# A gated cross-attention and expert layer: queries completed on TensorE, the last chunk's output path in two halves

## The reference

```
x = x + tanh(g_xattn) * attention(layernorm(x), ctx, ctx)      # 8 heads of 4 columns, softmax over 1601 keys, then Wo, bo
x = x + tanh(g_ffn)   * experts(layernorm(x))

experts(x2): scores = softmax(x2 @ router_w + router_b)        # 8 experts
             G, idx = top_k(scores.T, 512)                     # each expert takes its 512 best rows
             h1 = relu(x2[idx] @ w1 + b1);  eo = h1 @ w2 + b2  # 256 -> 1024 -> 256
             y[idx] += eo * G
```

## Time and profile before

| | |
|---|---|
| median of 3 runs | 636.62 us (634.16 to 638.63) |
| the profiled execution | 634.5 us, of which its span is 632.7 us |
| busy in the span | TensorE 542.0 us (86%), VectorE 449.5 (71%), ScalarE 387.8 (61%), GpSimd 187.8 (30%) |
| VectorE's maxima, L866 | 256 reductions, 243.2 us |
| mean granted TensorE clock | 0.928 of 2.4 GHz |

### The profile page before, as it was taken

One profiled execution on the slowest core, in us unless ns is written; L12 is line 12 of the kernel. 1 busy time (PEld: TensorE's weight loads), 2 busy tenths in 40 slices (PEclk: granted clock), 3 DMA queues, 4 the chain that ended last, 5 costly groups with the idle time before them and its releaser, 6 DMA issues.

```text
span 632.7 us, 12435 instructions
## 1 busy us (share of the span) xinstructions
PE 542.0 (86%) x4879; PEld 326.5 (52%) x4879; DVE 449.5 (71%) x815; ACT 387.8 (61%) x742; POOL 187.8 (30%) x184
## 2 busy tenths in 40 slices
PE   5876999989999899999889843369999999999991
PEld 3421333334334343433334332249898898898981
DVE  4789979997798987989895037735767667666630
ACT  1673878876888768888687810025646646655641
POOL 3053420040510315100092001050526437346223
PEclk9995999998999999999899955559999999999996
DMA  7600000000000000000000050021446347346123
GB/s 265 221 2 1 1 1 2 2 2 34 2 35 1 3 34 1 35 2 1 35 36 1 1 171 29 2 66 34 142 122 137 102 108 188 98 107 157 20 26 33
DMA packets 23469, 35.74 MB, mean 56 GB/s; under 512 B 3411, under 2 KB 16116, under 8 KB 23284
## 3 DMA queue, kind: packets, MB, share of 16 engines
q1 hardware_dynamic: 17268, 26.56, 12.6%
q0 software_dynamic: 6144, 8.39, 7.6%
HBM read 26.56 MB, written 8.39 MB: 55 GB/s over the span
## 4 chain that ended last, share of the span: by engine, by line
PE 58%; DVE 23%; issue 5%; ACT 5%; POOL 1%; DMA 0%; POOLq 0%; DVEq 0%; ACTq 0%
DVE mquart L866 16%; PE ps L1424 14%; PE ps L1431 14%; PE ps L1265 9%; PE ps L1235 5%; PE ps L1252 4%; ACT probs L647 3%; PE ps L1172 2%; PE ps L1383 1%; PE ps L1302 1%; PE ps L1288 1%; PE ps L1397 1%; PE ps L1406 1%; DVE stats L775 1%; PE ps L1273 1%
## 5 line engine op out<-in xcount | busy, mean ns | idle before, releaser
L866 DVE TENSOR_REDUCE mquart<-ps 128x2 f32<-128x802 f32 x256 | 243.2, 988 | 23.5 <-PE ps L1235 18.1
L647 ACT ACTIVATE probs<-ps 128x512 f32<-128x512 f32 (+1 forms) x416 | 222.3, 598 | 57.1 <-PE ps L1252 56.0
L1265 PE MATMUL ps<-probs,vp 128*32 128x256 f32 (+1 forms) x1664 | 135.1, 397 | 4.3 <-ACT osb L556 4.3
L1235 PE MATMUL ps<-kpad,qrows 64*128 64x401 bf16 x512 | 91.8, 346 | 15.2 <-DVE mquart L866 14.3
L1113 DVE TENSOR_TENSOR h1l<-hf,h1h 128x512 fp32r<-128x512 f32 x64 | 44.1, 689 | 72.5 <-ACT hf L721 72.5
L1252 PE MATMUL ps<-qfull,kpad 64*128 64x256 bf16 (+1 forms) x832 | 89.1, 278 | 1.7 <-ACT xf L569 0.6
L720 ACT ACTIVATE h1h<-ps,b1T 128x512 fp32r<-128x512 f32 x64 | 44.0, 687 | 62.9 <-PE ps L1424 62.8
L1431 PE MATMUL ps<-w2h,h1h 128*128 128x256 f32 x256 | 73.8, 288 | 1.4 <-DVE h1l L1113 0.7
L1431 PE MATMUL ps<-w2l,h1h 128*128 128x256 f32 x256 | 72.4, 283 | 0.0
L1431 PE MATMUL ps<-w2h,h1l 128*128 128x256 f32 x256 | 72.3, 283 | 0.0
L1235 PEld LDWEIGHTS ps<-kpad,qrows 64*128 64x128 bf16 x512 | 26.2, 94 | 76.8 <-DVE mquart L866 39.3
(11 more groups left out here) (163 smaller groups left out, 677.8 us busy)
## 6 DMA issues: line engine op xcount, KB each, us to landing
w1raw<-in_L_ffn_w SPq DMA_DIRECT2D x16, 512.0 KB, 4.1
w2raw<-in_L_ffn_w SPq DMA_DIRECT2D x16, 512.0 KB, 4.5
xs<-in_x SPq DMA_DIRECT2D x4, 512.0 KB, 8.7
out<-xs SPq DMA_DIRECT2D x4, 512.0 KB, 2.6
x_rows<-x SPq DMA_DIRECT2D x4, 512.0 KB, 2.6
ctx_sb<-in_ctx SPq DMA_DIRECT2D x3, 512.0 KB, 6.8
b2b<-in_L_ffn_b SPq DMA_DIRECT2D x1, 1024.0 KB, 11.6
toks<-x_rows,idx_get POOLq DMA_INDIRECT x32, 2.8
```

The source lines that it names most:

```text
L647: nc.scalar.activation(out_p, ps[0:w, next_bank(), :], ACT.Exp, scale=float(SCALE)).then_inc(s_ex, 1)
L866: nc.vector.tensor_reduce(mquart[:, t, a, :, kq], ps[:, b:b + 2, 0:MAXW], AX.X, ALU.max).then_inc(s_mr, 1)
L1235: last = mm(ps[:, bank + b, 0:MAXW], qrows[band(b), g, q:q + P], kpad[band(b), g, a, lo:lo + MAXW], start=True, stop=True)
L1265: last = mm(ps[32 * hh:32 * hh + 32, PV, 0:UW], vp[0:w, kt, g, hh, :], probs[0:w, step % PROBS, hh, :], start=(kt == 0), stop=(kt == NKT - 1))
```

## The change

- `place_max` first multiplies the identity with qrows into the bank (bf16, 256 columns) and adds the transposed maxima on top; `q_full` becomes a ScalarE copy. The placing uses one of ScalarE's three banks.
- `max_parts` reduces twice, into mparts (bf16) and into nmax, instead of reducing once and copying; mquart has two buffers.
- Unit 0 follows the first 16 maxima at once; its loop spreads 20 tiles instead of 16 (`tiles_by(0, i)`).
- wo and the router of chunks 0 to 2 run in two halves at two steps, in ScalarE's banks. ScalarE scales wo's result into x2 (`scale_wo`), GpSimd adds it to x (`add_wo`); ScalarE takes the logits (`take_L`), GpSimd adds the router's bias (`add_rb`).
- LayerNorm-1 statistics of chunks 1 and 2 move before the first maxima, with their rstd on GpSimd ahead of add_bo(0); those of chunk 3, and LayerNorm-2's, are spread over four steps.
- One key projection and the query projection of group 1 are cut in two, with a maximum between.
- The last chunk's output path runs in two halves of two tiles: the first inside the last unit (HALF_O and the names beside it give the steps; the transposing of b1 goes there too), the second behind it. Its stores come in halves.

```diff
+            if u == 0:
+                return TILES + (tiles_by(1, -1) - TILES) * (i + 1) // (2 * NKT)
             return min(TILES * UNITS, TILES * (u + 1) + TILES * (i + 1 + 2 * LEAD) // (2 * NKT))
 
...
-        O_THIS, O_LAST, BACK_AT, WO_AT = (2, 4), (0, 4), (0, 7), (0, 10)
+        O_THIS, O_LAST, BACK_AT, WO_AT = (2, 4), (0, 4), (0, 7), ((0, 10), (0, 12))
...
-        X2_AT, ROUTER_AT = ((2, 6), (2, 8)), (2, 11)
+        X2_AT, ROUTER_AT = ((2, 6), (2, 8)), ((2, 10), (2, 12))
+        LAST = NC - 1
+        HALF_O, HALF_BACK, HALF_WO, HALF_B1, HALF_X2, HALF_ROUTER = [(UNITS - 1, k) for k in (2, 3, 5, 8, 10, 12)]
...
+            for half in range(2):
+                t = CT * LAST + UQ * half
+                sp.wait_ge(s_x1, LAST + half + 1)
+                sp.dma_start(out_v[:, t:t + UQ, :], xs[:, t:t + UQ, :]).then_inc(s_out1, 16)
+                sp.wait_ge(s_x2, LAST + half + 1)
+                sp.dma_start(x2_v[:, t:t + UQ, :], x2[:, UQ * half:UQ * half + UQ, :]).then_inc(s_x2st, 16)
...
+            def add_rb(c):
+
+                pool.wait_ge(s_rwts, 64)
+                pool.wait_ge(s_lgr, 2 * (c + 1))
+                rows = lg[:, CT * c:CT * c + CT, :]
+                nc.gpsimd.tensor_tensor(rows, rows, rbb[:, :].unsqueeze(1).to_broadcast([P, CT, E]), ALU.add).then_inc(s_lg, 1)
...
+            def add_wo(c):
+
+                pool.wait_ge(s_xb, c + 1)
+                pool.wait_ge(s_wt, 2 * (c + 1))
+                rows = xs[:, CT * c:CT * c + CT, :]
+                nc.gpsimd.tensor_tensor(rows, rows, x2[:, :, :], ALU.add).then_inc(s_x1, 1)
...
+            rstd_1(1)
+            rstd_1(2)
             pool.wait_ge(s_bob, 1)
             add_bo(0)
...
                 if c + 1 < NC:
-                    rstd(c + 1, mv1, rstd1, s_mv1, s_ve1, s_rs1)
+                    if c + 1 == NC - 1:
+                        rstd_1(c + 1)
                     ln1_apply(c + 1)
                     add_bo(c + 1)
+                if c > 0:
+                    add_wo(c - 1)
+                if c + 1 < NC:
...
+                    rstd_2(c - 1)
                     ln2_apply(c - 1)
+                if 0 < c < LAST:
+                    add_rb(c - 1)
             first_weights()
-            rstd(NC - 1, mv2, rstd2, s_mv2, s_ve2, s_rs2)
+            add_rb(LAST - 1)
+            for half in range(2):
+                rstd_2(LAST, half)
...
+            def q_full(u):
+
+                c, g, h, r = unit(u)
+                act.wait_ge(s_mpl, u + 1)
+                at_least(act, s_sc, 2 * NKT * (u + 1 - PER_CHUNK))
+                take(qfull[:, g, UW * h:UW * h + UW], ps[:, next_bank(), 0:UW], s_qf)
+
+            def scale_wo(c, half, bank):
+
+                act.wait_ge(s_W, 2 * c + half + 1)
+                act.wait_ge(s_x2st, 16 * (c + 1))
+                at_least(act, s_X, KD * c)
+                nc.scalar.activation(x2[:, 2 * half:2 * half + 2, :], ps[:, bank, :].rearrange("p (t d) -> p t d", d=D), ACT.Copy,
+                                     scale=tg[:, 0:1]).then_inc(s_wt, 1)
+
...
+            def take_L(c, half, bank):
+
+                act.wait_ge(s_R, 2 * c + half + 1)
+                t = CT * c + UQ * half
+                take(lg[:, t:t + UQ, :], ps[:, bank, 0:UQ * E].rearrange("p (t e) -> p t e", e=E), s_lgr)
...
+                    if kt == PLACE and u + 1 < UNITS:
+                        q_full(u + 1)
...
-            take_N(NC - 1, 4)
+            take_N(LAST, 1, 4)
             take(iota_x[:, :, :], cst[:, C_IOTA:C_IOTA + P].unsqueeze(2).to_broadcast([P, P, QT]), s_iota)
-            for k in range(KD):
-                take_X(NC - 1, k, k)
+            take_X_half(1, 0)
...
+                if j == 0:
+                    for t in range(CT):
+                        ln1_stats(1, t)
+                if j == 1:
+                    ln1_aggr(1)
+                    ln1_stats(2, 0)
+                if j == 2:
+                    for t in range(1, CT):
+                        ln1_stats(2, t)
+            ln1_aggr(2)
             split(4, 0, CW, 0, qrows[:, 0, 0:CW])
...
-                nc.vector.tensor_reduce(nmax[:, :, :].rearrange("p t (b a) -> p t a b", a=2), mquart[:, :, :, :, :], AX.X, ALU.max,
+                at_least(dve, s_mpl, u)
+
+                def spread(t, row):
+                    return t[:, :, :, row].rearrange("p t (b a) -> p t a b", a=2)
+
+                nc.vector.tensor_reduce(spread(mparts, KROW_M), mquart[:, u % 2, :, :, :, :], AX.X, ALU.max, negate=True)
+                nc.vector.tensor_reduce(nmax[:, :, :].rearrange("p t (b a) -> p t a b", a=2), mquart[:, u % 2, :, :, :, :], AX.X, ALU.max,
                                         negate=True).then_inc(s_nm, 1)
                 dve.wait_ge(s_nm, u + 1)
-                at_least(dve, s_mpl, u)
-                nc.vector.tensor_copy(mparts[:, :, :, KROW_M], nmax[:, :, :]).then_inc(s_mhi, 1)
-                dve.wait_ge(s_mhi, u + 1)
                 nc.vector.tensor_tensor(mparts[:, :, :, KROW_M + 1], nmax[:, :, :], mparts[:, :, :, KROW_M], ALU.subtract).then_inc(s_mp, 1)
...
-                nc.vector.tensor_tensor(qfull[:, g, UW * h:UW * h + UW], ps[:, next_bank(), 0:UW], qrows[:, g, a:a + UW], ALU.add).then_inc(s_qf, 1)
...
-                nc.vector.scalar_tensor_tensor(rows, ps[:, bank:bank + 2, :].rearrange("p b (t d) -> p (b t) d", d=D), tg[:, 0:1], rows,
...
-            for n in range(TILES, TILES + 2):
-                max_tile(n)
-            q_full(0)
-            for n in range(TILES + 2, TILES + EARLY):
-                max_tile(n)
...
-                    if c > 0 and r == 1 and kt == 1:
-                        ln2_stats(c - 1, FIRST2)
-                    if c > 0 and r == 1 and kt == 2:
-                        ln2_stats(c - 1, LAST2)
-                    if c > 0 and r == 1 and kt == 3:
+                        normalise(c - 1, 1, 0, next_bank())
+                    if c > 0 and (r, kt) in LN2_AT:
+                        ln2_stats(c - 1, LN2_AT.index((r, kt)))
+                    if c > 0 and (r, kt - 1) == LN2_AT[-1]:
                         ln2_aggr(c - 1)
...
+                    if c + 1 == NC - 1 and (r, kt) in LN1_AT:
+                        ln1_stats(c + 1, LN1_AT.index((r, kt)))
+                    if c + 1 == NC - 1 and (r, kt - 1) == LN1_AT[-1]:
                         ln1_aggr(c + 1)
-            c = NC - 1
-            nc.vector.tensor_copy(low_bf[:, :], cst[:, C_LOW:C_LOW + P])
-            nc.vector.tensor_copy(ones_bf[:, :], cst[:, C_ONE:C_ONE + P])
-            nc.vector.tensor_copy(iota_b[:, :], cst[:, C_IOTA:C_IOTA + P])
-            normalise(c, 1, 3)
...
+                    if (u, kt) == (UNITS - 1, 0):
+                        nc.vector.tensor_copy(low_bf[:, :], cst[:, C_LOW:C_LOW + P])
+                        nc.vector.tensor_copy(ones_bf[:, :], cst[:, C_ONE:C_ONE + P])
+                        nc.vector.tensor_copy(iota_b[:, :], cst[:, C_IOTA:C_IOTA + P])
+                    if (u, kt) == HALF_O:
+                        normalise(LAST, 1, 0, next_bank())
+                    if (u, kt) == HALF_WO:
+                        residual_half(0, next_bank())
+                        second_norm_half(0)
+                    if (u, kt) == HALF_B1:
+                        take_b1(next_bank())
+                    if (u, kt) == HALF_ROUTER:
+                        take_L_half(0, next_bank())
+            normalise(LAST, 1, 1, 3)
+            residual_half(1, 5)
+            second_norm_half(1)
+            take_L_half(1, 2)
+
+            dve.wait_ge(s_lg, NC + 1)
+            dve.wait_ge(s_out1, 16 * (NC + 1))
+            dve.wait_ge(s_x2st, 16 * (NC + 2))
...
-                bank = next_dve((s_qf, u + 1))
+                bank = next_act((s_qf, u + 1))
+                mm(ps[:, bank, 0:UW], ident_bf[:, :], qrows[:, g, q:q + UW], start=True, stop=False, skip_group_check=True)
                 for t in range(UQ):
-                    last = mm(ps[:, bank, P * t:P * t + P], mparts[:, t, :, :].rearrange("p h r -> p (h r)"), ident_bf[:, :], start=True, stop=True)
+                    last = mm(ps[:, bank, P * t:P * t + P], mparts[:, t, :, :].rearrange("p h r -> p (h r)"), ident_bf[:, :],
+                              start=False, stop=True, skip_group_check=True)
                 last.then_inc(s_mpl, 1)
...
+            def wo(c, half, bank):
+
+                pe.wait_ge(s_Nt, part_of(c, half) + 1)
+                for t in range(UQ * half, UQ * half + UQ):
+                    last = mm(ps[:, bank, D * (t % 2):D * (t % 2) + D], onT[:, P * t:P * t + P], wo_sb[:, :], start=True, stop=True)
                 last.then_inc(s_W, 1)
...
+                if n == FIRST_KEYS[0]:
+                    third = next_act((s_xf, 8))
+                    k_project(2, 1, third, (0,))
+                if n == FIRST_KEYS[0] + 1:
+                    k_project(2, 1, third, (1,))
...
             place_max(0)
-            for n in range(TILES + 2, TILES + EARLY):
```

(22 more changed lines are left out.)

306 lines of the change are left out of this document (157 added, 149 removed).

## The result

The changed kernel takes 619.55 us (median of 4 runs, 616.31 to 620.54) against 636.69 (634.16 to 638.63) for the one before: ratio 0.9724 [0.9675, 0.9774], 17.1 us less. The forecast was 617 us. Its profiled execution took 620.54 us, with a span of 618.7 (before 632.7) and a mean granted clock of 0.932 (before 0.928).

A forecast was written before the change was run, and what follows sets the result against it. VectorE was taken to bound plain units, TensorE Q units and experts, mutual waits the end. Savings 3.0 + 0.5 + 5.8 + 0.5 + 3.6 + 5.3 = 18.7 us off the profiled 634.5 give 615.8; forecast 617 us, range 609 to 628.

The forecast's parts named there:

- Part 1: Maxima and q_full in the attention units: freeing VectorE saves 3.0 us in plain-like units, 0.5 us in Q units.
- Part 2: Output projection, residual, router and statistics leaving VectorE: 5.8 us in three wo units (2.6 if dips stay), router 0.5 us.
- Part 3: Start: units begin 4.4 us sooner, four maxima added to unit 0 cost 0.8; 3.6 us saved, from 1 to 6.
- Part 4: End: chain to the logits 7.6 us shorter, last unit 2.0 longer, 0.3 for waits; 5.3 us saved, from 1 to 7.
- (a): Rival: ScalarE's three-bank ring and TensorE give little back; 10 us saved, 625 us; chance 0.24 together with rival (c).
- (d): Rival: the q_full copy in ScalarE's order makes exps wait; slower, 645 us; chance 0.04.
- (b): Rival: TensorE's gaps close in all sixteen units, last unit hides all its additions; 10 us more, 607 us; chance 0.10.
- I expect the split wo, with its waits gone, to spare them: Wo units: splitting wo avoids the 3.3 us stretches at 1.2 GHz in two units, each costing TensorE 1.6 us.
- may wait up to 1 us: Second wo unit: transposes at step 9 wait for GpSimd's normalised rows, as LN1 statistics end two steps later.
- the last of the 16 maxima so ends where it did: Start: 1.25 us of moved statistics on the path, against 1.2 us saved by cutting the first projections in two.
- about 1.3 are hidden: Last unit: of the first half's 3.3 us on TensorE, 1.3 hide in slack and 2.0 lengthen the unit.
- rival (c): First half not ready when the last unit ends, tail waits; Part 4 gives nothing, 622 us; chance 0.24 together with (a).

The follow-up runs named there:

- (1): Changed kernel with the placing back in VectorE's banks and VectorE adding qrows into q_full again; 623.46 us, ratio 0.9778.
- (3): Changed kernel with wo of chunks 0 to 2 as one block in VectorE's banks and VectorE adding it to x; 619.75 us, ratio 0.9726.
- (8): Changed kernel with the edits of (1) and (3) together; 624.92 us, ratio 0.982.
- (2): Changed kernel with the last chunk's output path whole behind the last unit, no steps of it inside that unit; 620.9 us, ratio 0.9746.
- (5): Changed kernel with LayerNorm-1 statistics of chunk 3 moved from unit 8 to unit 1; 616.66 us, ratio 0.9676.
- (4): Changed kernel with the group-1 key and query projections in one piece again; 619.79 us, ratio 0.9734.
- (6): Changed kernel with LayerNorm-1 statistics of chunks 1 and 2 moved from the start into units 0 and 1; 617.51 us, ratio 0.9694.
- (7): Changed kernel with added matmuls that nobody reads, keeping TensorE busy before unit 0; 618.19 us, ratio 0.9705.
- (11): Changed kernel with (7)'s matmuls, chunk 2's statistics in unit 1, chunk 3's in unit 6, and 16 maxima in unit 0, 20 in unit 1; 618.04 us, ratio 0.9701.

## Why the prediction was right, and where it wasn't

By the two profiles, before and after, against the terms of the sum:

```
                                        predicted   profiles   what undoing it showed
four plain units and unit 13                 3.0        4.5     3.7 (1)
Q units                                      0.5        0.8     0.8 (1)
output-projection units 4, 8, 12             5.8        4.8     wo alone 0.4 (3), with q_full 2.8 (8)
router units                                 0.5        0.6
start and unit 0                             3.6        0.7     1.4 by more profiles
last unit                                   -2.3       -3.6    -3.5 (2)
tail                                         7.6        6.5     5.3 (2)
sum                                         18.7       14.3
```

Behind rmax another 0.4 us is lost; the spans differ by 14.0. The medians differ by 17.1, since the profiled execution of after is the highest of its four and that of before lies 2.2 under its median (it has two dips behind unit 0; the second profile of before, at 637.91 us, has four). So the total was right, 17.1 for 18.7, and in part by luck: profile against profile it is 14.3, in which part 1 gave 1.8 us more than forecast and parts 2, 3 and 4 gave 0.9, 2.9 and 2.4 less.

**Part 1** was right in mechanism and place: TensorE's two waits went, the unit stopped at TensorE (15.08 of 15.40 us), and ScalarE's exps did not wait for the copy. They wait less: for scores they stand 21.9 us between 50 and 357 us, instead of 49.6. The group by form, changed kernel:

```profile
L703 ACT ACTIVATE probs<-ps 128x512 f32<-128x512 f32 x384 | 205.8, 599 | 24.6 <-PE ps L1357 21.9
```

Rivals (a) and (d) are out, and so is (b): the last unit hid none of its additions. I had left TensorE's slot of the ring 0.2 us too dear: 15.6 forecast, 15.38 measured.

**Part 2** came near in its sum by wrong reasons. The step that failed is "I expect the split wo, with its waits gone, to spare them": the split is worth 0.4 us, and with it undone no dip appears (3). One came back when placing, q_full and wo were all undone (8), in one of three units of one profile. What spares the dips stays open: two of the seven seen stand behind the router's whole block, which only the kernel before has and which no experiment made whole again. Their price was right, 1.4 measured for 1.6. Of the rest of unit 4, the moved statistics are most. The wait that I named for unit 8, "may wait up to 1 us", was 1.29 us, and taking the statistics out of that unit gave 2.26 (5); unit 8 is the one unit with wo that got slower. The Trainium skill, TensorE: Matmul & The Clock Gate, section "What's actually happening", has a freely running activity window, and by it I held the dips for something that may come back in any run. The trace agrees as to the place: units 4 and 12 in one profile of before, 6, 8, 12 and 14 to 15 in the other. It doesn't as to the kernel: no profile of the changed kernel has a dip in units 1 to 15, and of its variants only experiment 8.

**Part 3** is the weakest term. Timeline of the start of the changed kernel, answering to the earlier trace rows:

```profile
34.55 2.07 PE L1248 MATMUL ps<-ctxT,wkr 128*128 128x512 f32 x2
...
36.84 1.12 PE L1248 MATMUL ps<-ctxT,wkr 128*128 128x512 f32 x2
...
43.21 1.89 PE L1272 MATMUL ps<-xnT,wqr 128*128 128x512 f32 x2
...
47.58 2.79 DVE L968 TENSOR_REDUCE mquart<-ps 128x2 f32<-128x802 f32 x3 [1.00 <-PE ps L1336]
...
50.73 0.20 DVE L984 TENSOR_TENSOR mparts<-nmax,mparts 128x8 bf16<-128x8 f32 x1
...
52.24 0.61 PE L1357 MATMUL ps<-qfull,kpad 64*128 64x256 bf16 x4 [0.47 <-ACT qfull L612]
```

The block behind the maxima went as forecast (0.20 us instead of 2.27), and from the last of the first 16 maxima to the scores it is 1.9 us. The first scores came at 52.24 instead of the forecast 51; "the last of the 16 maxima so ends where it did" failed: 50.37 instead of 48.5 (in the second profile of the changed kernel it held: 48.5, and first scores at 50.17). TensorE ran three of the four halves of the cut projections at 1.2 GHz (1.8 to 2.1 us for two matmuls that take 1.12 in the second half of the keys), and VectorE waited for them. The cut, put at 1.2 us, shows no gain (4), and the statistics, put at 1.25 us on the path, cost 2.1 by the one profile without them (6). Then "0.8" for four maxima in unit 0 was mis-sized: unit 0 grew by 2.5 us. Windows of unit 0, the kernel before first, then the changed one:

```profile
55.40:77.50 22.10, 21.04 (x218) 7.63 (x214) 20.75 (x32) 16.98 (x33) 8.50 (x7) 0.82 0.01 1
52.20:76.80 24.60, 22.70 (x227) 8.25 (x227) 21.40 (x26) 17.51 (x34) 11.80 (x10) 0.83 0.01 1
```

The clock was as low before, so it alone is not the growth. But before it cost nothing that shows (22.05 us at 0.82, 22.03 at 0.88 in the second profile), and with four more maxima on TensorE a full clock takes 1.85 us off the unit (7). At full clock four maxima more or less in unit 0 are worth 1.05 us (11). Over the six profiles with this start (after, the changed kernel once more, 1, 2, 3 and 5) unit 0 ends at 76.0 us on average against 77.35 in the two of before: 1.4 us, not 3.6.
The Trainium skill, SBUF — State Buffer, section "SBUF: two separate sides", has the lock that GpSimd and some VectorE operations take for a whole instruction. The trace agrees in this kernel too: the same operation takes 0.20 us at 50.73, when GpSimd's addition of bo has not begun (it comes at 54.64).

**Part 4**: the wrong term is "about 1.3 are hidden". Last unit and tail of the changed kernel, timeline, answering to the earlier trace rows:

```profile
340.99 1.12 PE L1394 MATMUL ps<-wo_sb,onT 32*128 32x256 f32 x4
...
347.07 0.66 PE L1407 MATMUL ps<-cst,x 128*128 128x128 f32 x4
...
349.80 1.06 PE L1412 MATMUL ps<-rw_sb,x2T 128*128 128x8 f32 x8
...
351.93 0.38 ACT L612 ACTIVATE osb<-ps 128x256 f32<-128x256 f32 x1 [1.64 <-PE ps L1370]
...
354.25 2.07 PE L1394 MATMUL ps<-wo_sb,onT 32*128 32x256 f32 x4 [0.46 <-ACT onT L612]
356.35 0.75 DVE L1004 SCALAR_TENSOR_TENSOR xs<-ps,tg,xs 128x512 f32<-128x512 f32 x1 [3.02 <-PE ps L1394]
...
361.99 1.87 PE L1412 MATMUL ps<-rw_sb,x2T 128*128 128x8 f32 x8 [0.69 <-ACT x2T L612]
363.90 0.17 DVE L1035 TENSOR_TENSOR lg<-ps,rbb 128x16 f32<-128x16 f32 x1 [3.77 <-PE ps L1412]
```

TensorE waits for no step of the first half, so rival (c) is out; but the unit was TensorE's already (11.60 of 12.20), and its work went in at full price. The tail's links came as forecast but for wo's half, 2.07 us at 1.2 GHz instead of 1.3. A half costs 1.12 at full clock in the last unit, and the tails of 11.24 us against those of 12.2 to 12.4 are of that size. Undone (2), the end gives 1.6 to 1.8 us, a third of the 5.3; the profiles of before and after show 3.0 since before's wo also ran into the clock drop (2.99 us, in experiment 2 1.99).

## What to carry to other kernels

Price added work by the engine that sets the stage: in a unit where TensorE's rows fill 95% of the time, 3.6 us of TensorE work cost 3.5, and the idle time of the other engine is not room (four maxima cost VectorE's full 3.85 us beside 3.6 us of its idle time). When work that feeds a slower engine is spread out to relieve one, follow the last piece through that engine to the step where its result stands in the order: four statistics that ended two steps later made TensorE stand 1.29 us, and taking them out of the unit gave 2.26. And undo parts in pairs too: one alone cost 4.1, the other 0.4, both together 5.4, with a clock dip that the one profile of either alone does not have.

## What the runs showed of the hardware that I had not expected

- TensorE's clock fell to 1.2 GHz for some 3.3 us amid units in which TensorE is busy 19 to 21 us of 21 to 23. Behind unit 0 and before the last osb copy it did so in all three profiles of kernels that have the placing and the output projection in VectorE's banks (units 4 and 12; 6, 8, 12 and, for 6.8 us, 14 to 15; 12), and in none of the eleven others. Its price is 1.4 to 1.5 us each time, 2.1 for the long one.
- Each of these seven dips begins at most 1.5 us behind the end of an unbroken block of small matmuls of 1.95 to 2.0 us: five behind wo's eight, two behind the router's sixteen (190.14 us, where the block that starts at 188.19 ends, and 347.15). But three such blocks of wo in experiment 3 have none behind them. The kernel before alone has whole blocks of the router, so which of the things that it has together brings the dips about, banks, wo or router, isn't settled; a run with the router alone whole again would tell more.
- The start differs between executions of the same code by more than most edits are worth: the first maximum comes between 30.25 and 33.47 us in the fourteen profiles, and from 32.07 to 30.25 for the kernel before alone. Single profiles can't price an edit there.
